# Cross attention's guard moved into the gated experts of a two-layer decoder

## The chip, the cores and the metric

One core of one Trainium2 chip runs the whole program. The metric is the device time of one execution in microseconds, as a median over runs. PE is TensorE, ACT ScalarE, DVE VectorE, POOL GpSimd, SP SyncE, which here only issues transfers.

## What is computed

x has 32 batches of 128 tokens of 128 channels, fp32. Two layers run one after the other, each of an attention, a second attention and a mixture of experts, each added to x. What matters here is the second attention and the first experts:

```
attn = clip(q @ k.T * scale, -1e4, 1e4)
attn = softmax(attn)
attn = where(any(isnan(attn)), 1/Nkv, attn)     # over the whole tensor
x = x + (attn @ v) @ Wo + bo                    # cross attention
x = x + experts(layernorm(x))                   # 8 gated, top 2, and 2 shared experts
```

If any probability is not a number, every output of cross attention becomes the mean of the values, projected. The kernel computes that replacement always, and chooses it by a flag.

## The kernel before

The program is a sequence of blocks. In each, every engine has its own instruction stream, joined to the others by semaphores; between blocks all engines meet. x stays in SBUF as 128 x 4096 (x_all), in 8 groups of 4 batches, 512 columns each. PSUM has 8 banks of 512 columns.

The blocks: the setup, `attention` for self and cross attention together, `uniform_guard` (line 788), `gated_experts` (line 875), `attention` again (causal), `latent_attention`, and `relu_experts` (line 1277), which ends the program.

**In attention** the order on each engine is written out in a table of steps with leads (`ORDERS`, `AHEAD`). SP (lines 778 to 785) copies each group of x into `x_before` as soon as self attention's output is in it, and loads the context of each group. POOL adds the output's bias to x (`add_bias`, L710) after the group has been normalised and, in cross attention, copied. VectorE adds each batch's projected output to x (`add_output`, L663). It also sums the keys and the remainders (`key_sums`, `lo_sums`), from which the guard takes the mean and the flag.

**The guard** runs by itself between the two blocks. It splits the key sums in a rounded and a remaining part (L816, L820), multiplies by the value weights (L845 to L847), makes the mean (ACT, L869) and splits it again, projects it and adds the bias (L831). PE then spreads each batch's row over 128 tokens, one matmul (two passes) per batch, four batches per bank (L861); VectorE adds each bank to `x_before` (L836); and at last one predicated copy of 4096 columns (L840) puts `x_before` in x's place if the flag is set.

**The gated experts** first round their weights (ACT, L1050) and take the remainder (VectorE, L1227). They go by slots: slot n works on group n's five expert pairs (NB = 5, k = 0 to 4), while group n+1 is transposed, split and routed, group n+2 gets its moments and is normalised, and group n-1 is finished. Per k: PE `up` (six matmuls, L950 to L952), `spread_gate` (L977), `down` (L987); ACT silu and a copy of the gate; VectorE their product (L1124); POOL the product with the gate (L1241). The routing is 20 small VectorE operations per group (L1143 to L1174), with one power on POOL in the midst (L1259). PE turns the gates (`transpose_gates`, L1011) at the end of the slot before, ahead of the group's first `up`. Slots -2 to 1 and 6 to 8 are written out; slots 2 to 5 are a loop of two passes over two slots. The bank TR takes the transposes of both x and y; two banks each (H1, H3) take the experts' inputs.

**The end.** The experts of the second layer scatter their weighted rows to `returned` in DRAM, 512 B per row. When all have landed, SP reads them back in 16 transfers (per group and choice, 256 KB each in 512 B pieces, L1454), VectorE adds them to x (L1420, 16 adds), and SP stores the 8 groups (L1458).

## Time and profile before

| | |
|---|---|
| median of 3 runs | 1429.71 us (1428.98 to 1429.92) |
| the profiled execution | 1422.62 us, its span 1420.8 us |
| busy share: PE, DVE, ACT, POOL | 84%, 62%, 48%, 54% |
| mean granted TensorE clock | 0.912 of 2.4 GHz |
| self and cross attention end | 529.49 us |
| guard | to 552.3 us |
| gated experts, last addition to x | 704.49 us |
| last experts, first read of their rows | 1398.67 us |

The table says where the stages lie; how full each is, the windows say. A time in the text is one on the clock of this span.

### The profile page before, as it was taken

Reading aid. Unit: us, or ns where it says so; the run is one execution under the profiler, and the core shown is the slowest. Engines: PE = TensorE matmul, PEld = TensorE weight load, DVE = VectorE, ACT = ScalarE, POOL = GpSimd, SP = SyncE. Lnnn points to the kernel's source line nnn. Section 1 sums busy time; section 2 is a strip of 40 time slices with the busy share of each in tenths; the row PEclk is TensorE's granted clock in tenths of the full one; section 3 lists DMA queues with packets and bytes.
Section 4 is the critical chain, followed back from the end, with each engine's and each line's share of the span. In section 5 each row is a group of like instructions: output and inputs, shape, how many; then the busy total and the mean of one; then the engine's idle time right before and its main releaser. Section 6 shows DMA issues by size and latency. Waiting matters only on the chain. (4 is left out here: it accounts for less than half of the span.)

```text
span 1420.8 us, 34474 instructions
## 1 busy us (share of the span) xinstructions
PE 1192.8 (84%) x12734; PEld 904.7 (64%) x12734; DVE 877.0 (62%) x2007; ACT 675.0 (48%) x1298; POOL 767.3 (54%) x870
## 2 busy tenths in 40 slices
PE   1899998888888875899889999994999994199992
PEld 0577776655555554566457777764899984188881
DVE  3487877589999974666446666555888855022223
ACT  1345544444544531555345454437888532056561
POOL 3677775555566520444365566525776657444552
PEclk9999999789999995999979999996999965599996
DMA  9910000000000000000000000000000001256656
GB/s 347 381 65 10 2 2 15 1 15 28 15 15 8 1 2 1 0 1 0 0 1 3 2 3 2 2 2 23 12 13 2 15 29 49 94 186 206 199 188 181
DMA packets 58865, 75.44 MB, mean 53 GB/s; under 512 B 13246, under 2 KB 40003, under 8 KB 58448
## 3 DMA queue, kind: packets, MB, share of 16 engines
q1 hardware_dynamic: 53328, 63.72, 13.9%
q0 software_dynamic: 4544, 8.47, 1.7%
q8 instruction: 103, 1.69, 0.5%
q10 hardware_dynamic: 832, 1.09, 0.2%
q14 instruction: 58, 0.48, 0.1%
HBM read 40.37 MB, written 31.70 MB: 51 GB/s over the span
## 5 line engine op out<-in xcount | busy, mean ns | idle before, releaser
L590 DVE TENSOR_REDUCE maxes<-bank 128x8 f32<-128x1024 f32 x192 | 234.3, 1221 | 56.3 <-PE bank L392 54.6
L520 ACT ACTIVATE self_probs<-bank 128x1024 f32<-128x1024 f32 x128 | 129.1, 1022 | 46.0 <-PE bank L424 45.6
L1428 POOL DMA_INDIRECT returned<-relu_y,relu_slots x78 | 76.7, 983 | 93.6 <-DVE relu_y L1403 81.1
L1371 ACT ACTIVATE relu_hidden<-bank,cols 128x256 f32<-128x256 f32 x156 | 74.0, 474 | 98.1 <-PE bank L1329 98.1
L527 ACT ACTIVATE self_neg_max<-bank 128x512 fp32r<-128x512 f32 x64 | 38.2, 597 | 155.1 <-PE bank L438 155.1
L731 POOL TENSOR_TENSOR self_k_hi_m<-self_kq_hi,const 128x512 fp32r<-128x512 f32 x64 | 66.6, 1040 | 81.2 <-ACT self_kq_hi L548 81.2
L1329 PE MATMUL bank<-relu_s,relu_w_tile 128*128 128x256 f32 x312 | 94.3, 385 | 0.5 <-DVE relu_s L1397 0.5
L1337 PE MATMUL bank<-relu_hidden,relu_w_tile 128*128 128x256 f32 x312 | 92.9, 381 | 0.0
L1397 DVE COPY relu_s<-bank 128x256 f32<-128x256 f32 x39 | 16.6, 424 | 122.1 <-PE bank L1319 122.1
L600 DVE RECIPROCAL self_recip<-bank 128x128 f32<-128x128 f32 x64 | 61.2, 956 | 32.1 <-PE bank L451 29.8
L596 DVE TENSOR_SCALAR bank<-bank 128x1024 f32<-128x1024 f32 x64 | 78.2, 1223 | 3.3 <-PE bank L412 3.3
L2214 POOL DMA_INDIRECT routed<-latent_rows,latent_place_i x64 | 62.4, 975 | 24.4 <-issue 16.6
L451 PE MATMUL bank<-self_probs,values 128*32 128x128 f32 x2048 | 74.0, 288 | 1.4 <-ACT self_neg_max L527 1.2
L731 POOL TENSOR_TENSOR causal_q_lo_m<-causal_kq_lo,const 128x512 fp32r<-128x512 f32 x32 | 33.3, 1041 | 73.1 <-PE bank L424 73.0
L451 PE MATMUL bank<-self_probs,head_ones 128*32 128x128 f32 x2048 | 71.5, 282 | 0.0
L424 PE MATMUL bank<-self_neg_max,const_r 32*128 32x512 f32 x256 | 63.2, 485 | 9.7 <-DVE bank L596 6.3
L731 POOL TENSOR_TENSOR self_q_lo_m<-self_kq_lo,const 128x512 fp32r<-128x512 f32 x64 | 66.6, 1041 | 2.7 <-PE bank L424 2.7
L451 PEld LDWEIGHTS bank<-self_probs,values 128*32 128x32 f32 x2048 | 55.5, 114 | 18.9 <-issue 16.1
L520 ACT ACTIVATE causal_probs<-bank 128x1024 f32<-128x1024 f32 x64 | 64.5, 1022 | 5.1 <-PE bank L424 2.6
L438 PE MATMUL bank<-ident,maxes 128*128 128x128 f32 x384 | 66.0, 297 | 0.8 <-POOL maxes L754 0.3
L731 POOL TENSOR_TENSOR self_q_hi_m<-self_kq_hi,const 128x512 fp32r<-128x512 f32 x64 | 66.6, 1040 | 0.0
L1337 PEld LDWEIGHTS bank<-relu_hidden,relu_w_tile 128*128 128x128 f32 x312 | 59.5, 191 | 8.3 <-ACT relu_hidden L1371 0.2
(380 smaller groups left out, 3474.9 us busy)
## 6 DMA issues: line engine op xcount, KB each, us to landing
relu_w_tile<-in_w_ffn SPq DMA_DIRECT2D x39, 512.0 KB, 3.4
routed<-blank SPq DMA_DIRECT2D x1, 19760.0 KB, 60.6
relu_slots<-routed SPq DMA_DIRECT2D x39, 130.0 KB, 3.0
relu_back<-returned SPq DMA_DIRECT2D x16, 256.0 KB, 4.5
x_all<-in_x SPq DMA_DIRECT2D x8, 256.0 KB, 8.3
x_before<-x_all SPq DMA_DIRECT2D x8, 256.0 KB, 2.8
out_x<-x_all SPq DMA_DIRECT2D x8, 256.0 KB, 4.2
self_ctx_in<-in_ctx SPq DMA_DIRECT2D x8, 192.0 KB, 2.6
```

The source lines that it names most:

```text
L424: mm = pe.matmul(t_bank(u), cr[rows_of(u), C_ONES + u * P:C_ONES + (u + 1) * P], neg_max[n % 2][rows_of(u), :], start=False, stop=True, sk ...
L438: mm = pe.transpose(OM[:, j * P:(j + 1) * P], maxes[n % 2][:, j * P:(j + 1) * P], sb["ident"][:, :])
L451: mm = pe.matmul(OM[rows_of(u), c:c + P], of(u, j), probs[n % 2][:, u, j, :], start=j == 0, stop=j == U - 1)
L520: act.activation(probs[n % 2][:, 2 * pair:2 * pair + 2, :, :].rearrange("p u j q -> p (u j q)"), T[:, 2 * pair * GT:(2 * pair + 2) * GT], ...
L590: dve.tensor_reduce(out.rearrange("p j u -> p u j"), S.rearrange("p (u j k) -> p u j k", u=2, j=U), AX.X, ALU.max, negate=True).then_inc(m ...
L596: dve.tensor_scalar(t, t, CLAMP / scale, -CLAMP / scale, ALU.min, ALU.max).then_inc(clipped, 1)
L731: pool.tensor_tensor(out[n % 2][:, :, :], src[(n // GB) % 2][:, batch_cols(n)].bitcast(F32).unsqueeze(1).broadcast_to([P, U, P]), slots.un ...
L1329: pe.matmul(HT[i % 2][:, 0:TT], w_tile[t % NW][:, c * P:(c + 1) * P], s[t % 2][:, :], start=True, stop=True)\
L1337: pe.matmul(YT[t % 2][:, 0:TT], w_tile[t % NW][:, F1 + c * P:F1 + (c + 1) * P], hidden[i % C1][:, :], start=c == 0, stop=c == C1 - 1).then ...
L1371: act.activation(hidden[i % C1][:, :], HT[i % 2][:, 0:TT], ACT.Relu, bias=sb["cols"][:, bass.ds(r + (COL_RELU + c), 1)]).then_inc(hidden_d ...
L1428: pool.indirect_dma_start(returned[:, :], bass.IndirectOffsetOnAxis(ap=slots[t % NX][:, b, P:P + 1].bitcast(I32), axis=0), y[t % NY][:, b, ...
L2214: pool.indirect_dma_start(routed[:, :], bass.IndirectOffsetOnAxis(ap=place_i[u % 3][:, k, b:b + 1], axis=0), rows[G % 4][:, k, n % GB, :], ...
```

## The change

1. `uniform_guard` is gone. In attention, ACT ends its program by rounding the key sums (`key_hi`), POOL by taking the remainder (`key_lo`) and the zeros of the flag. VectorE's sums now signal `keys_summed`.
2. SP copies group G to `x_before` after POOL has added the bias, in the order: context G+1, copy of G; each copy waits for the one before. POOL no longer waits for the copy; VectorE's `add_output` does.
3. `gated_experts` begins with the guard. PE makes the mean (into H1) and the flag's sums (H3), then spreads groups 0 to 3 straight from the mean: stationary one column of `v_mean` broadcast to 128, moving `w_out`, so that spreading and projecting are one matmul. They go to four banks that are still free (`EARLY`). VectorE makes the flag, and adds groups 0 and 1 from PSUM; ACT copies groups 2 and 3 to SBUF (`keep_mean`) and POOL adds them (`add_mean`). Groups 4 to 7 are spread in slots 0 to 3 into TR, with the same copy and addition.
4. VectorE chooses a group (`choose`, 512 columns) just before its moments. The weights' remainder is taken after the first moments, and not ahead of all.
5. Group 0's first expert `up` comes ahead of its gates' transpose; that, and two spreads of the gate, come after the second `up`.
6. The loop is written out: `run` is one plain loop over the slots -2 to 8.
7. At the end: `returned` has another order of rows (token p, batch b at p * 32 + b), so that a partition's rows are contiguous; it is read in 8 transfers of 512 KB in pieces of 4 KB, the first choice by SP and the second by ACT; the stores go by SP and ACT in turn.

```diff
@@ attention
+            if "cross" in kinds:
+                act.wait_ge(keys_summed, NG)
+                act.activation(sb["key_hi"][:, :], sb["key_sums"][:, :], ACT.Copy).then_inc(keys_rounded, 1)
...
+                if kind(n) == "cross":
+                    dve.wait_ge(x_kept, 16 * (n // GB - G0 + 1))
                 dve.tensor_tensor(x_of(n), PB[:, 0:P], x_of(n), ALU.add).then_inc(pb_read, 1)
...
             def add_bias(G):
                 pool.wait_ge(xn_done, G + 1)
-                if of_group(G) == "cross":
-                    pool.wait_ge(x_kept, 16 * (G - G0 + 1))
...
+                    if G > 0:
+                        sp.wait_ge(biased, G0 + G)
+                        if G > 1:
+                            sp.wait_ge(x_kept, 16 * (G - 1))
+                        sp.dma_start(x_group(G - 1, "x_before"), x_group(G - 1)).then_inc(x_kept, 16)
@@ gated_experts
+    EARLY = [YT, GATE, H1[1], H3[1]]
...
         def run(engine, slot):
-            for n in range(-2, 2):
+            for n in range(-2, NG + 1):
                 slot(0, n)
-            with engine.Fori(0, 2) as it:
-                for n in range(2, 4):
-                    slot(it, n)
-            for n in range(6, NG + 1):
-                slot(0, n)
...
+            def mean_of_values():
+                pe.wait_ge(ones_set, 1)
+                pe.matmul(H3[0][:, 0:2 * NG], ones[:, :], sb["zeros"][:, :], start=True, stop=True).then_inc(bad_spread, 1)
+                split_matmul(H1[0][:, 0:B], (sb["w_hi"][0:DC, wv:wv + P], sb["w_lo"][0:DC, wv:wv + P]),
+                             (sb["key_hi"][:, :], sb["key_lo"][:, :])).then_inc(mean_made, 1)
+
+            def spread_mean(G):
+                if G == 0:
+                    pe.wait_ge(mean_copied, 1)
+                if G >= len(EARLY):
+                    pe.wait_ge(x_lo_done, G - 2)
+                out = EARLY[G] if G < len(EARLY) else TR
+                for b in range(GB):
+                    n = GB * G + b
+                    mm = pe.matmul(out[:, b * P:(b + 1) * P], v_mean[:, n:n + 1].broadcast_to([P, P]), w_out,
+                                   start=True, stop=True)
+                mm.then_inc(y_spread, 1)
...
+                        if n == 0 and k == 1:
+                            transpose_gates(it, n)
+                            spread_gate(it, n, 0)
+                        if k < NB - 1 and (n, k) != (0, 0):
                             spread_gate(it, n, k)
...
+                    if k == 2 and n >= 0 and there(it, n + 4):
+                        spread_mean(n + 4)
...
+            mean_of_values()
+            for G in range(len(EARLY)):
+                spread_mean(G)
             run(pe, slot)
...
+            keep_mean(2)
+            keep_mean(3)
             run(act, slot)
...
+            def choose(G):
+                columns_of = slice(G * GT, (G + 1) * GT)
+                before = sb["x_before"][:, columns_of]
+                if G < 2:
+                    dve.wait_ge(y_spread, G + 1)
+                    dve.tensor_tensor(before, EARLY[G][:, :], before, ALU.add).then_inc(y_first, 1)
+                    dve.wait_ge(y_first, G + 1)
+                else:
+                    dve.wait_ge(y_added, G - 1)
+                dve.copy_predicated(X[:, columns_of], flag[:, :].broadcast_to([P, GT]), before).then_inc(chosen, 1)
...
+            def add_mean(G):
+                pool.wait_ge(y_mean_read, G - 1)
+                before = sb["x_before"][:, G * GT:(G + 1) * GT]
+                pool.tensor_tensor(before, before, y_mean[G % 2][:, :], ALU.add).then_inc(y_added, 1)
...
+                    if k == 3 and n >= 0 and there(it, n + 4):
+                        add_mean(n + 4)
                     if k >= 1 and there(it, n):
                         gate_hidden(it, n, k - 1)
...
+                    if k == 1 and n == -2:
+                        add_mean(2)
+                        add_mean(3)
@@ relu_experts
+        def load_back(queue, k):
+            rows = returned[k * B * P:(k + 1) * B * P, :].rearrange("(p b) d -> p (b d)", p=P)
+            for H in range(NG // 2):
+                part = slice(2 * H * GT, 2 * (H + 1) * GT)
+                queue.dma_start(back[k][:, part], rows[:, part]).then_inc(back_in[H], 16)
...
+            load_back(act, 1)
+            for G in range(1, NG, 2):
+                store(act, G)
...
+            load_back(sp, 0)
+            for G in range(0, NG, 2):
+                store(sp, G)
```

## Rows read from the trace of the kernel before

**Rows 1.** Windows: length; busy PE, PEld, DVE, ACT, POOL; PEclk; DMA share; GB/s
```profile
529.50:532.80 3.30, 1.05 (x8) 0.83 (x8) 1.32 (x8) 0.52 (x2) 0.21 (x1) 1.00 0.00 0
...
532.80:539.00 6.20, 6.19 (x29) 6.20 (x30) 2.08 (x3) 0.00 (x0) 0.00 (x0) 0.51 0.00 0
...
560.00:571.10 11.10, 3.81 (x16) 3.35 (x16) 5.67 (x30) 2.48 (x6) 2.21 (x3) 0.50 0.01 1
...
589.60:606.10 16.50, 16.50 (x69) 10.31 (x69) 11.01 (x36) 8.68 (x16) 7.25 (x7) 1.00 0.00 0
...
655.40:671.60 16.20, 16.20 (x69) 10.29 (x68) 11.10 (x36) 8.68 (x16) 7.28 (x7) 1.00 0.00 0
```

**Rows 2.** Timeline of the attention's end and the guard: start, us, engine, line, operation
```profile
529.20 0.29 DVE L663 TENSOR_TENSOR x_all<-bank,x_all 128x128 f32<-128x128 f32 x1 [0.58 <-PE bank L464]
...
531.25 0.29 ACT L869 ACTIVATE guard_v_mean<-bank,cols 128x32 f32<-128x32 f32 x1 [6.26 <-PE bank L852]
...
532.81 13.99 PE L861 MATMUL bank<-guard_y,ident 32*128 32x128 f32 x64 [0.37 <-DVE guard_y L831]
...
536.59 0.69 DVE L836 TENSOR_TENSOR x_before<-bank,x_before 128x512 f32<-128x512 f32 x1 [1.01 <-PE bank L861]
...
547.63 4.68 DVE L840 COPY_PREDICATED x_all<-bank,x_before 128x4096 f32<-128x4096 int32 x1
```

**Rows 3.** Timeline of the gated experts' beginning, the same columns
```profile
553.99 1.49 DVE L1227 TENSOR_TENSOR ffn_w_lo<-raw_ffn,ffn_w_hi 128x1280 fp32r<-128x1280 f32 x1 [1.68 <-ACT ffn_w_hi L1050]
...
555.48 0.86 DVE L1184 BATCH_NORM_STATS2 ffn_stats<-x_all 128x6 f32<-128x128 f32 x4
...
558.59 1.65 ACT L1071 ACTIVATE ffn_xn<-x_all,ffn_shift_ln,ffn_rstd 128x128 f32<-128x128 f32 x4 [4.63 <-DVE ffn_shift_ln L1194]
...
568.61 1.65 ACT L1071 ACTIVATE ffn_xn<-x_all,ffn_shift_ln,ffn_rstd 128x128 f32<-128x128 f32 x4 [6.51 <-DVE ffn_shift_ln L1194]
...
570.02 0.16 DVE L1165 TENSOR_TENSOR ffn_two<-ffn_e_second,ffn_two 128x4 f32<-128x4 f32 x1
...
571.17 1.02 PE L1011 MATMUL bank<-ident,ffn_gate_parts 128*16 128x128 f32 x4 [5.57 <-DVE ffn_gate_parts L1174]
...
571.84 0.77 PE L950 MATMUL bank<-ffn_x_hi,ffn_w_hi 128*128 128x512 f32 x1
...
572.22 0.59 ACT L1050 ACTIVATE ffn_g_parts<-bank 16x512 fp32r<-16x512 f32 x1 [1.97 <-PE bank L1011]
...
577.14 0.27 PE L950 MATMUL bank<-ffn_w_hi,ffn_x_hi 128*128 128x8 f32 x1
```

**Rows 4.** Timeline of the second slot, then a line of waits
```profile
601.53 1.29 POOL L1241 TENSOR_TENSOR ffn_hidden<-ffn_product,ffn_gate 128x512 f32<-128x512 f32 x1 [0.22 <-PE bank L987]
...
601.58 1.26 DVE L1165 TENSOR_TENSOR ffn_two<-ffn_e_second,ffn_two 128x4 f32<-128x4 f32 x1
...
PEld bank L1011 <- DVE ffn_gate_parts L1174: 3.0, 5, 0.7
```

**Rows 5.** Timeline of cross attention, then a DMA issue of the page
```profile
487.77 1.28 POOL L710 TENSOR_TENSOR x_all<-x_all,rows 128x512 f32<-128x512 f32 x1
...
513.97 0.29 DVE L663 TENSOR_TENSOR x_all<-bank,x_all 128x128 f32<-128x128 f32 x1 [0.65 <-PE bank L464]
...
x_before<-x_all SPq DMA_DIRECT2D x8, 256.0 KB, 2.8
```

**Rows 6.** Timeline of the end of the program
```profile
1398.67 11.92 SPq L1454 DMA_DIRECT2D relu_back<-returned  x16
...
1402.24 1.42 DVE L1420 TENSOR_TENSOR x_all<-x_all,relu_back 128x512 f32<-128x512 f32 x2 [7.92 <-DMA relu_back<-returned]
...
1409.82 5.95 DVE L1420 TENSOR_TENSOR x_all<-x_all,relu_back 128x512 f32<-128x512 f32 x8 [0.33 <-DMA relu_back<-returned]
```

**Rows 7.** Windows of the loads at the beginning and of the stores at the end
```profile
20.00:40.00 20.00, 9.69 (x26) 6.03 (x26) 6.10 (x21) 5.04 (x11) 7.96 (x13) 1.00 1.05 385
...
1415.80:1418.00 2.20, 0.00 (x0) 0.00 (x0) 0.00 (x0) 0.00 (x0) 0.00 (x0) 0.50 1.15 344
```


## What is expected, and why

> **What bounds the kernel now.** The page's busy shares first (in the table above): PE 84% of the span, VectorE 62%, so work that leaves PE idle is worth removing, and work added to PE where PE is full costs its own length. Then the table of windows [rows 1], to see which of the two holds where the change acts. In the guard (532.8 to 539) PE is full, but at a granted clock of 0.51, the lower of its two levels (1.2 GHz), with only the spreading matmuls in it; from 560 to 571.1, while the first group of the gated experts is routed, PE works 3.8 of 11.1 us at 0.50; in the second group's slot (589.6 to 606.1) PE is busy 16.50 of 16.50 us at 1.00 (2.4 GHz). The four windows after it (16.2 to 16.5 us, the last one shown) are as full. So three stages with three limits: a serial chain (529.5 to about 577), PE (577 to 700), and, at the end of the program, transfers and VectorE's adds (from 1398.7).
>
> **The chain now** [rows 2]. Attention ends at 529.49. The means of the values stand at 531.54. Spreading them over the eight groups takes PE 13.99 us, 1.71 per group; VectorE adds each (0.69) and then chooses all at once in 4.68. Only at 552.3 does the block end, and the gated experts begin [rows 3]: weights split until 555.5, moments at 555.48, normalised x from 558.59, gates ready just before their transpose at 571.17, first expert at 571.84, and the logits' matmuls of the second group from 577.14.
>
> **Change 1: guard inside the gated experts.** Up to 531.54 nothing is saved: the mean still waits for the ones that POOL writes (the flag is now worked out beside it) [rows 2]. From there:
> - First spread: four matmuls of the same output size. 1.71 us at clock 0.50 [rows 2]; PE had 1.00 from 529.5 to 532.8 [rows 1], so half of that, 0.85: done at 532.5. The add 0.69 and an eighth of the choice, 4.68/8 = 0.59 [rows 2], give 534.0 for the first moments instead of 555.48 [rows 3]: 21.5 us earlier.
> - Moments to normalised x took 3.1 us (555.48 to 558.59) [rows 3]: 537.1 at best. Four things now stand in that gap. On VectorE the weight split, 1.49 + 0.16 [rows 3], lies between moments and shift, but beside POOL's power, which has the shift wait for 2.9 us anyway: 0. On ACT the copies of the means of groups 2 and 3 stand ahead of the normalisation; the fourth spread ends between 535.0 (four at 0.85) and 538.4 (at 1.71), with a copy of 0.6 like that at 572.22 [rows 3], so 535.6 to 539.0. On POOL two additions, 1.3 each like its multiplication [rows 4], follow the power. A small VectorE operation beside such a POOL operation takes its length: the product of four columns at 570.02 took 0.16 with POOL idle, the same line at 601.58 took 1.26 and ended with POOL's multiplication [rows 3, 4]. The shift is such an operation, and POOL's addition is queued right behind the power that releases it: one (538.4) or two (539.6) can go first. I take 539.2 for the normalisation, ends 537.1 and 541: 19.4 us earlier.
> - By the Trainium skill (SBUF — State Buffer, Who interferes with whom) that is an exclusive lock between GpSimd and VectorE instructions with two SBUF inputs, and it binds both ways. The rows above agree with the one direction; none shows the other.
> - Then the chain as before: gates ready 12.5 us after the normalisation begins [rows 3]. The second group's add and choice (0.69 + 0.59) and its moments stand on VectorE ahead of the routing, beside the logits' matmuls that it waits for: twelve matmuls in 2.7 us at the lower clock. 0, or 0.2.
>
> **Change 2: the first expert before the gates.** The first expert's six matmuls (2.6 at the lower clock: 571.84 to the next work at 574.3, the last of them faster) now run under the routing. But next on PE's queue is the transpose of the second group, which waits for its normalisation, 10.0 us after the first (568.61 less 558.59) [rows 3] plus 1.65; everything behind it waits too. So: 11.7, transpose 0.7 to 1.1, second expert 1.4 (clock 1.00) to 2.6 (0.50), gates' transpose, ACT copy, spread, ACT copy, spread 3.2 to 3.5 with PE idle between: second logits at 17.0 to 18.9 after the normalisation, before 18.55 (577.14 less 558.59) [rows 3]. The reordering gives 1.5 to -0.3, and the lower clock could cost those logits another 1.3. I take 18.1, 0.4 gained. Front in sum: 557.3 instead of 577.1, **-19.8** (ends -23.0 and -16).
>
> **Change 3: four spreads, copies and adds in four slots.** In slots 0 to 3 PE is full, so each spread costs 0.85 there. Its ACT copy (0.6) falls under the next expert. POOL's addition (as long as a multiplication, 1.29) comes ahead of the third expert's multiplication, which is done when the fourth's begins at 601.53 [rows 4]. The last routing steps are VectorE operations that wait behind POOL as above, and PE already waits for them: 3.0 us in the five slots from 589, 0.7 at most [rows 4]. Followed through: the last multiplication then runs until 603.9, and the product of four columns ends with it instead of at 602.84; the gates are 1.1 later while PE comes 0.85 later. So 1.1 per slot, **+4.4** for four; 3.4 if the routing finds gaps, 8.8 if it loses one more POOL operation in each. The choice of a group (0.59) is in six slots on VectorE, 11.0 busy of 16.5 [rows 1], in the gap before the logits: 0.
>
> **Change 4: the loop written out.** The four looped slots keep the pace of the others (16.2 to 16.5), so **-0.2**, between 0 and -0.5.
>
> **Change 5: x kept after the bias is added, and VectorE waits for it.** SP's copy of a group now follows that group's bias on POOL. The last bias is at 487.77, the first output of that group is added at 513.97, and a copy lands 2.8 us after its issue [rows 5]: 22 us to spare, so 0. The context load of a group is queued behind a copy two groups older, whose bias comes earlier still: 0. The rounding of the key sums stands at the end of ACT's and POOL's programs, while VectorE still has the last outputs to add: 0.
>
> **Change 6: the end.** Now one queue issues 16 loads in 11.92 us, one per 0.75, and the first store waits behind them; VectorE's first add is at 1402.24, 3.6 after the first issue, for 0.5 MB, and its last eight take 5.95, 0.74 each [rows 6]. From 1398.7 on 6.29 MB move (24 transfers of 256 KB) in 512 B pieces, at 344 GB/s where nothing else binds. The transfers at 20 to 40 us, in long pieces, went at 385 GB/s [rows 7]. New: two queues, 4 KB pieces, first pair of 1 MB after 2.2 + 2.7 (3.6 less 1.4 for 0.5 MB, and 1 MB at 385) = 1403.6; 16 adds of 0.74 end at 1415.5, last store 0.75 issue + 2.5 to land: 1418.8. By data: 4.19/385 + 2.10/344 = 17.0 us from 1399.6, 1416.6, which is earlier. So **-2.0**; 0 if the first pair comes 2 us later, -3.2 if the last store lands in 1.3. The new scatter addresses change no size: 0. The Trainium skill (DMA: Bandwidth & Descriptors, Issuing engines are not separate DMA queues) has all queues on the same 16 engines, so that a second one saves only issue time; by its limit of HBM per core, about 358 GB/s, the loads would take 11.7 us instead of 10.9, against 385 measured here.
>
> **Sum.** -19.8 + 4.4 - 0.2 - 2.0 = -17.6 us. The profiled execution took 1422.62 (span 1420.8 and 1.8 around it): 1405.0. The three timed runs have a median of 1429.71, 7.1 above it, which the trace doesn't place; taken off there: **1412.1**.
>
> **Rivals.**
> - POOL's power is held by the weight split (1.49), which starts while the power is due: the normalisation is 1.4 later, 1413.5. For it: the order on VectorE, and that POOL can hold VectorE in this way [rows 3, 4]. Against it: no row shows POOL held. Chance 0.25. The Trainium skill's rule (SBUF — State Buffer, Who interferes with whom) would have it so.
> - The slots cost more: one more POOL operation before the routing's end in each slot, 8.8 instead of 4.4, and the second expert at the lower clock, +1.7: 1418.2. For it: PE already waits 0.6 per slot for the gates. Chance 0.13.
> - Front at its fast end: no addition before the shift and clock 1.00 for the spreads: -3: 1409. Chance 0.17.
> - The change does less than it says: if a fifth and later spread had to be done before the experts begin, each would cost 1.7; the code puts four ahead. 1419; 0.02.
> - Slower: in cross attention the wait for the kept copy. If each copy were issued only when the group's first output is due, VectorE, with the maxima of the next batch queued behind, would stand 2.8 us and PE behind it, eight times: +22.4, 1434.5. It decides from 2.2 us per group. Against it 22 us of slack. Chance 0.02.
> - The forecast: 0.40; another 0.01 that all cancels.
>
> Range: 1406.5 (fast front with a fast end of the program) to 1418.5. A measurement of this kernel tells about 0.2% (2.9 us) from no change: faster 0.97, same 0.01, slower 0.02.
>
> **What would show it.** First moments near 534 and normalisation near 539 after an unchanged 529.5; second logits near 557; slots 0 to 3 of about 17.5 us and slots 4 and 5 of 16.4; additions on POOL right before VectorE's long small operations; last adds ending near 1415.3 less the shift. Wrong would be: a normalisation after 541, slots over 18.5, or an attention stage that ends later than 530.

## The result, and the profile after

The changed kernel takes 1424.25 us (median of 20 runs, 1419.47 to 1443.25) beside 1434.53 us for the kernel before in the same comparison (median of 20): a ratio of **0.9932, 95% interval 0.9917 to 0.9947**, or 9.7 us less (the medians lie 10.3 apart). A few runs at a much lower mean clock stand outside the ratios: here the one of 1443.25 us (clock 0.865), later one of `unrolled` (1987.85) and one of `after_third` (1433.27). The forecast was 1412.1 us, 17.6 less: the direction holds, the size is little more than half. The profiled execution took 1423.83 us, its span 1422.0.

The guard's place in the trace after, beside [rows 2, 3]. Columns: start, us, engine, line, operation, out<-in.

```profile
531.23 0.61 PE L942 MATMUL bank<-zeros,ffn_ones 128*128 128x16 f32 x2 [1.32 <-POOL ffn_ones L1294]
...
532.51 0.29 ACT L1089 ACTIVATE ffn_v_mean<-bank,cols 128x32 f32<-128x32 f32 x1 [6.67 <-PE bank L885]
...
532.85 5.87 PE L955 MATMUL bank<-w_out,ffn_v_mean 128*128 128x128 f32 x32 [0.38 <-ACT ffn_v_mean L1089]
535.04 0.69 DVE L1173 TENSOR_TENSOR x_before<-bank,x_before 128x512 f32<-128x512 f32 x1 [2.80 <-PE bank L955]
535.76 0.73 DVE L1177 COPY_PREDICATED x_all<-ffn_flag,x_before 128x512 f32<-128x512 int32 x1
536.53 0.87 DVE L1186 BATCH_NORM_STATS2 ffn_stats<-x_all 128x6 f32<-128x128 f32 x4
...
537.84 1.46 DVE L1206 TENSOR_TENSOR ffn_w_lo<-raw_ffn,ffn_w_hi 128x1280 fp32r<-128x1280 f32 x1
...
538.11 1.25 POOL L1263 TENSOR_SCALAR ffn_var_eps<-ffn_mean_var 128x4 f32<-128x4 f32 x1 [6.86 <-DVE ffn_mean_var L1190]
...
539.44 1.04 POOL L1266 TENSOR_TENSOR ffn_rstd<-ffn_var_eps,ffn_power 128x4 f32<-128x4 f32 x1
540.45 2.48 POOL L1277 TENSOR_TENSOR x_before<-x_before,ffn_y_mean 128x512 f32<-128x512 f32 x2
540.51 1.22 DVE L1196 SCALAR_TENSOR_TENSOR ffn_shift_ln<-ffn_mean_var,ffn_rstd 128x4 f32<-128x4 f32 x1 [1.13 <-POOL ffn_rstd L1266]
541.76 0.88 ACT L1041 ACTIVATE ffn_xn<-x_all,ffn_shift_ln,ffn_rstd 128x128 f32<-128x128 f32 x2 [2.41 <-DVE ffn_shift_ln L1196]
```

Attention ends at 530.24 in this trace, 0.75 later than in the one before. The first moments are at 536.53 instead of 555.48, the first normalisation at 541.76 instead of 558.59, the second logits' products at 559.80 instead of 577.14. Two operations of four columns are long here: POOL's addition to the variances (1.25) beside VectorE's split of the weights, and VectorE's shift (1.22) beside POOL's addition of the mean.

The granted clock of this stretch and of the beginning of causal attention, in the trace after. Columns: window, length, busy PE (instructions), PEclk, DMA share, GB/s.

```profile
529.10:532.60 3.50, 1.74 (x7) 0.67 0.00 0
532.80:536.50 3.70, 3.65 (x17) 0.50 0.00 0
536.50:541.80 5.30, 2.22 (x17) 0.94 0.00 2
...
694.50:700.50 6.00, 0.78 (x4) 0.75 0.01 3
700.50:712.50 12.00, 7.90 (x26) 0.50 0.00 0
712.50:718.50 6.00, 5.44 (x19) 0.50 0.00 0
718.50:724.50 6.00, 6.00 (x38) 0.50 0.01 3
724.50:736.50 12.00, 12.00 (x78) 0.50 0.00 1
736.50:742.50 6.00, 6.00 (x78) 0.55 0.01 3
```

The same windows of causal attention in the kernel before, counted from its first moments at 704.8:

```profile
704.80:710.80 6.00, 0.76 (x4) 0.68 0.00 0
710.80:722.80 12.00, 7.92 (x26) 0.50 0.00 1
722.80:728.80 6.00, 5.42 (x19) 0.50 0.00 0
728.80:734.80 6.00, 5.49 (x50) 0.83 0.01 3
734.80:752.80 18.00, 17.84 (x263) 1.00 0.01 3
```

TensorE's instructions are the same, in the same order, and for the first 24 us they start at the same times. Before, the clock then rises, 26 us in; after, it stays at 0.50 (1.2 GHz) for 21 us more, with PE busy 12.00 of 12.00 us. Nothing in causal attention was changed, and it is 8.4 us longer. No step of the forecast dealt with it.

The end of the program after, to be read beside [rows 6]:

```profile
1402.35 1.93 SPq L1339 DMA_DIRECT2D relu_back<-returned  x4
1402.36 2.05 ACTq L1339 DMA_DIRECT2D relu_back<-returned  x4
...
1407.54 10.84 DVE L1461 TENSOR_TENSOR x_all<-x_all,relu_back 128x512 f32<-128x512 f32 x16 [9.51 <-DMA relu_back<-returned]
```

Eight loads are issued in 2 us, the first addition comes 5.2 us after the first issue, and the sixteen run back to back.

**Stages.** Of each kernel that ran there is one trace; the names are explained with the experiments. The table has the stages of the two kernels, their repetitions and three with a part of the change (us; the first column runs from VectorE's last multiplication in cross attention, 1.2 ahead of its end, to the first moments of causal attention; the second to latent attention's beginning; the last from the first load of the returned rows to the end of the span).

| trace | guard and experts | causal | latent | last experts | end |
|---|---|---|---|---|---|
| before | 176.5 | 255.6 | 278.1 | 160.2 | 22.1 |
| before_again | 183.9 | 255.6 | 287.0 | 160.8 | 21.6 |
| tail_only | 183.7 | 255.5 | 290.8 | 160.6 | 19.6 |
| unrolled | 183.8 | 255.5 | 283.8 | 160.5 | 21.8 |
| after | 165.4 | 264.0 | 283.0 | 160.9 | 19.7 |
| after_again | 165.3 | 264.0 | 289.4 | 161.2 | 19.7 |
| after_third | 166.2 | 264.0 | 279.3 | 161.3 | 19.7 |
| front_only | 165.9 | 264.0 | 282.9 | 160.8 | 23.0 |

Latent attention takes 278 to 291 with the old front and 279 to 289 with the new, and explains nothing. The other columns give the change: 165.7 - 183.8 = -18.1 in the first (four traces with the new front, the three like ones with the old), +8.4 in the second, +0.5 in the fourth, -2.0 to -2.5 in the last: about -11.4, where the runs gave -9.7. (The first two traces, 1420.8 and 1422.0 in span, show no gain at all: the one of before is 7.3 short in the first column, and 4.8 are latent attention's.)

### The profile page after: what moved, and what is told of

It is laid out like the page before. It is cut to its first block and busy times, and to the rows that moved or that the text cites. A ratio compares the mean times of both kernels' runs of the same rounds, so it can differ in the third digit from the quotient of the medians.

```text
span 1422.0 us, 34178 instructions
## 1 busy us (share of the span) xinstructions
PE 1198.5 (84%) x12731; PEld 905.0 (64%) x12731; DVE 879.4 (62%) x2002; ACT 677.7 (48%) x1304; POOL 775.9 (55%) x878
## 5 line engine op out<-in xcount | busy, mean ns | idle before, releaser
L2249 POOL DMA_INDIRECT routed<-latent_rows,latent_place_i x64 | 62.9, 982 | 29.8 <-issue 16.9
L451 PEld LDWEIGHTS bank<-self_probs,values 128*32 128x32 f32 x2048 | 55.5, 115 | 19.2 <-issue 16.3
L438 PEld LDWEIGHTS bank<-ident,maxes 128*128 128x128 f32 x384 | 43.8, 148 | 33.8 <-issue 27.9
```

The lines of the kernel that those rows point to most:

```text
L438: mm = pe.transpose(OM[:, j * P:(j + 1) * P], maxes[n % 2][:, j * P:(j + 1) * P], sb["ident"][:, :])
L451: mm = pe.matmul(OM[rows_of(u), c:c + P], of(u, j), probs[n % 2][:, u, j, :], start=j == 0, stop=j == U - 1)
L2249: pool.indirect_dma_start(routed[:, :], bass.IndirectOffsetOnAxis(ap=place_i[u % 3][:, k, b:b + 1], axis=0), rows[G % 4][:, k, n % GB, :], ...
```

## The experiments

**Both kernels again, and the two halves of the change.**

> The kernel before, unchanged, for a second trace. Theory A (the half-clock stretch at the start of causal attention is chance): its length differs from the 24 us of the first trace by several us, and causal and latent attention together take other than 534.2 us (704.8 to 1239.0) by up to 10. Theory B (it belongs to the program): it is within 2 us of 24, and the two stages within 2 of 534.2. The time against the kernel before: ratio 1.000 in both.

> The changed kernel, unchanged, for a second trace. Theory A (chance): the half-clock stretch in causal attention isn't the 42 us of the first trace (700 to 742) and causal and latent attention take other than the 547.4 us there by up to 10. Theory B (moved there by the change): it is near 42 again and the two stages near 547. The stage of guard and gated experts takes 164.3 us (530.2 to 694.5) within 1.5 by both. Ratio 0.993 in both.

`front_only` is the changed kernel with the old end; `tail_only` is the old kernel with the new end:

```
-  sp: 16 loads relu_back[k][G] <- returned, then 8 stores      (L1454 before)
+  load_back(sp, 0), load_back(act, 1); store(sp, even G), store(act, odd G)
+  C_HOME: row of x numbered B * p + b instead of P * b + p
```

> The change without its last part: the rows are read back in 16 transfers by one queue and stored by it, as before. Theory A: the front alone is worth 11.0 us less 0.7 of attention, 0.9928; the end of the program takes 22.1 us as before. Theory B (part of the front's gain is given back in causal attention): 7 us, 0.995, and the half-clock stretch there is long again. If the end were worth nothing, this would be equal to the whole change, 0.993.

> The kernel before with only the last part of the change: rows in the new order, read in 8 transfers of 4 KB pieces by two queues, stored by two. Forecast by the windows: the end takes 19.6 instead of 22.1 us, ratio 0.9982. Rival (the rows scattered 16 KB apart slow the experts' loop or the last scatter): the loop is longer by 0.5 to 1 us and the ratio is 0.999 or above.

Ratios to before, in the order of the four texts above: 1.0019 [0.9999, 1.0039], 0.9934 [0.9907, 0.9961], 0.9927 [0.9901, 0.9953], 0.9983 [0.9962, 1.0004]. The gain is all but wholly the front's. The end is 2.0 to 2.5 us shorter in tail_only's own trace and 2.3 us in its median, at the edge of what these runs tell; with the new front the runs don't show it at all (front_only, without it, has 0.9927, the whole change 0.9934), though in the traces the end takes 23.0 us there and 19.7 with it. As to chance or program: causal attention's length is the program's, 255.5 or 255.6 in every trace of the table with the old front and 264.0 in every one with the new. The sums with latent attention, by which theory B was to be told too, missed (542.6 for 534.2 and 553.4 for 547.4), because latent attention alone differs by that much from trace to trace. And front_only met the time of its theory A with the long stretch of its theory B: the front is worth more than I thought, and causal attention takes it back.

The trace that the forecast rests on is the odd one of its kernel. In the first column it has 176.5, and the others 183.7 to 183.9: their clock rises later, and from the first to the second logits they take 16.9 instead of 13.0, from the second to the third 19.6 to 19.8 instead of 16.9. Their clock is lower from attention's end on. These are the windows of `before_again` and `tail_only` that answer to 529.5 to 532.8 in [rows 1], with the same columns (1.00 there; `unrolled` has 0.51 and `warm_before` 0.50):

```profile
532.97:536.27 3.30, 1.41 (x7) 1.35 (x8) 1.04 (x7) 0.52 (x2) 0.20 (x1) 0.58 0.00 0
...
524.61:527.91 3.30, 1.42 (x7) 1.36 (x8) 1.04 (x7) 0.52 (x2) 0.20 (x1) 0.51 0.00 0
```

**The loop alone** (`unrolled`):

```
-            for n in range(-2, 2): slot(0, n)
-            with engine.Fori(0, 2) as it: for n in range(2, 4): slot(it, n)
-            for n in range(6, NG + 1): slot(...)
+            for n in range(-2, NG + 1): slot(0, n)
```

> The kernel before with the gated experts' loop written out and nothing else. In the three traces with the old guard, causal attention lasted 255.5 to 255.6 us from its first moments to latent attention's beginning, and in the three with the new one 264.0. Theory P: the clock of TensorE at causal attention's beginning rises early or late by how the work lies in time, and written-out code alone doesn't move it: causal attention 255.6 us, and the whole within 0.1% of before (slots of the gated experts 0.0 to 0.2 us shorter at the two loop ends). Rival U: the written-out code is what moved it (its last slots run a little otherwise): causal attention 264.0, and the whole about 8 us slower than before (ratio 1.006).

Ratio 1.0003 [0.9985, 1.0021], causal attention 255.5, slots of 16.35 to 16.37 us from the second on (16.28 to 16.57 in the looped kernel). Theory P stands, U is out: written-out code neither costs nor gives anything, and it doesn't move the clock.

**Keeping TensorE at work in causal attention's beginning** (`warm_before` on the old kernel, `warm` on the new one):

```
+            def keep_warm(n):
+                for _ in range(n):
+                    pe.matmul(T[:, 3 * GT:4 * GT], cr[:, C_ID:C_ID + P], cr[:, 0:GT], start=True, stop=True)
+            # 20 ahead of step ("x", 0); 5, 3, 3, 5, 3 behind ("x",0) ("k",0) ("q",0) ("s0",0) ("x",1)
```

> The kernel before, with 39 products without use (128x128 by 128x512, into the bank that holds the key scores and is free until then) in TensorE's gaps at the beginning of causal attention: 20 ahead of the first transposes, 5, 3, 3, 5 and 3 later. Theory P: the granted clock stays at 1.00 there instead of 0.50 for 24 us, and causal attention falls from 255.6 to 246 to 250 us; whole ratio 0.993 to 0.997. Rival Q: products without use don't hold the clock, or cost as much as they give: 255 to 258 us.

> The changed kernel with the same 39 products at the beginning of causal attention. Theory P (the 8.4 us that causal attention lost are the clock's alone, 0.50 for 44 us instead of 24): causal attention falls from 264.0 to the same length as in the kernel before with these products, 246 to 250 us, within 0.5 us of it; ratio to before 0.981 to 0.985, some 12 to 17 us faster than the change alone. Rival Q (something else of the change slows causal attention): it falls by what the kernel before falls by, and stays 8 us longer than there.

`warm`: **0.9831 [0.9807, 0.9855]**, causal attention 250.0 us; once more (`warm_again`) 0.985 [0.9814, 0.9886] and again 250.0. No window of its first 56 us is below 1.00. So 14.0 us of causal attention come back by nothing but products whose result nobody reads: the 8.4 us are the clock's. `warm_before`: 0.9964 [0.9937, 0.9992], 254.6 us, where 246 to 250 were expected, and so not the same length as `warm` either. The low stretch wasn't gone but put off:

```profile
711.00:735.00 24.00, 21.83 (x133) 1.00 0.00 1
735.00:741.00 6.00, 5.84 (x58) 0.93 0.00 1
741.00:749.00 8.00, 8.00 (x90) 0.50 0.01 2
```

With the 39 products the clock stays up in four traces (`warm`, `warm_again`, `best`, `best2`: 250.0 us) and falls once, 29 us in and for 7 to 10 us, in four others (`warm_before`, `warm_late`, `late_add_warm`, `best2_again`: 253.0 to 254.6). What decides isn't explained; the kernel `best2` did both.

> The same kernel as warm, once more, beside the three above on one chip: the ratio to before 0.981 to 0.986 again, causal attention 250 to 253 us again. If causal attention were now 264, the 39 products had not been the cause.

**Split of the weights behind the shift** (`late_split`):

```
-                    if k == 0 and n == -2: split_weights()          # VectorE
+                    if k == 3 and n == -2: split_weights()
-                    if k == 1 and n == -2: add_mean(2); add_mean(3) # POOL
+                    if k == 1 and n == -1: add_mean(2); add_mean(3)
```

> The changed kernel with VectorE's split of the experts' weights behind the first shift instead of ahead of it, and GpSimd's first two additions of the mean one slot later, behind the second deviation. Theory L (the two engines keep each other from SBUF: GpSimd's addition to the variances took 1.25 us beside the split instead of 0.20, VectorE's shift 1.22 beside the addition instead of 0.16): both fall to 0.2 us, first moments to first normalisation takes 2.8 to 3.4 us instead of 5.2, and the first logits are read 2 us sooner after attention's end (17.2 instead of 19.2); whole ratio to before 0.990 to 0.993. Rival: the logits wait for the split instead, or the rounding of the weights on ScalarE ends later than the normalisation could begin: within 0.5 us of the change.

```profile
533.51 0.20 POOL L1263 TENSOR_SCALAR ffn_var_eps<-ffn_mean_var 128x4 f32<-128x4 f32 x1 [6.85 <-DVE ffn_mean_var L1190]
533.79 1.04 POOL L1266 TENSOR_TENSOR ffn_rstd<-ffn_var_eps,ffn_power 128x4 f32<-128x4 f32 x1
...
534.87 0.16 DVE L1196 SCALAR_TENSOR_TENSOR ffn_shift_ln<-ffn_mean_var,ffn_rstd 128x4 f32<-128x4 f32 x1 [1.54 <-POOL ffn_rstd L1266]
```

Theory L holds: 0.20 and 0.16 instead of 1.25 and 1.22, moments to normalisation 3.14 us instead of 5.23, first logits 17.6 us after the last multiplication of attention instead of 19.2. But the second logits come 32.4 us after it in both, since the two additions now hold the routing (two operations of 0.19 us took 1.01 and 1.18), and the stage is 167.1 us, 1.7 longer. The ratio is nevertheless 0.9885 [0.986, 0.9911], because causal attention took 255.6 us. Here is its clock:

```profile
691.60:693.60 2.00, 0.00 (x0) 1.00 0.03 8
693.60:715.60 22.00, 14.15 (x48) 0.50 0.00 0
715.60:719.60 4.00, 3.48 (x18) 0.76 0.00 0
719.60:723.60 4.00, 4.00 (x50) 1.00 0.02 4
```

So the long low stretch isn't tied to the new front either. In the twelve traces without warming products: where the clock fell 1.7 to 2.2 us after causal attention's first moments (before, before_again, tail_only, unrolled, late_split, late_add), it stayed low for 24 us; where it fell 2.9 to 3.1 us after (after, after_again, front_only, no_steady, spread_early, after_third), for 44. An edit 150 us earlier goes with one or the other; whether the moment of the fall is the cause or only a sign of it, and what sets it, isn't shown.

> The kernel late_split with the 39 products without use at the beginning of causal attention. Theory P (what causal attention lost or kept is the granted clock's alone): in late_split it had the shorter length already, 255.6 us, and with these products it comes to what the changed kernel had with them, 250.1 us, so the two edits together give less than their sum: 5.5 us more than late_split, a ratio to before of 0.982 to 0.986. Rival: the two add up in full (late_split's 8.4 us came from elsewhere): a ratio of 0.974 to 0.979.

`warm_late`: 0.9856 [0.9817, 0.9894], causal 253.0 instead of the 250.1 expected. The two edits don't add up, as P has it, though the clock was kept only up to the 29th us.

**What the slots cost.** `no_steady` leaves out the mean of groups 4 to 7; `spread_early`, built on `late_split`, makes their products ahead of the slots:

```
-                    if k == 2 and n >= 0 and there(it, n + 4): spread_mean(n + 4)   # both
-                    if k == 3 and n >= 0 and there(it, n + 4): add_mean(n + 4)      # no_steady alone
+  spread_early: spread_mean(4) behind transpose_x(0), spread_mean(5..7) behind up(0, 0); six y_mean tiles
```

> The changed kernel without the mean of groups 4 to 7: their products, their copy from the bank and GpSimd's addition are left out, so where the guard chose the replaced output these four groups would lack it; the predicated copies stay. It prices the slots. Theory T (the 1.16 to 1.9 us that each of slots 0 to 3 lost are TensorE's 0.9 us of spreading products, since TensorE bounds the slot, and the 0.5 us that it waits for gates held up by GpSimd's addition): without them slots 0 to 3 fall to 16.35 to 16.7 us, as slots 4 and 5 of the change, and the stage from attention's end to the first causal moments shortens by 4.5 to 5.5 us. Rival K: the predicated copy is what costs (it lengthens VectorE's order ahead of the routing), and the slots keep 0.8 us or more each of what they lost. The whole, with the granted clock's part of it open: ratio to before 0.984 to 0.991.

> The kernel late_split with the products of groups 4 to 7 made ahead of the steady slots, in TensorE's gaps of the beginning (one group behind the first transposes, three ahead of the second), each copied into a tile of its own; GpSimd's additions stay in slots 0 to 3. Theory T: slots 0 to 3 lose TensorE's 0.9 us each and keep up to 0.5 us of waiting for gates: 16.4 to 16.9 us instead of 17.7; the beginning keeps its length if the gaps are real (or grows by up to 1.5 us at the lower clock). Attention's end to the first causal moments 163 to 165 us instead of 167.1. Causal attention takes one of its two lengths (255.6 or 264.0) by how its beginning lies in time, which this theory can't place. Rival K: slots 17.3 or more, since the products weren't what they lost.

`no_steady`: slots 1 to 3 took 16.83, 16.64, 16.67 instead of 17.93, 17.71, 17.71, nearly as T has it; the stage didn't shorten (166.2), since slot 0 went at the lower clock (21.9 instead of 18.8), and the ratio is 0.9921 [0.989, 0.9951]. `spread_early`: 17.93, 17.70, 17.71, **unchanged though the products are gone**, so T falls. The stage is 172.9 us where 163 to 165 were expected, with a ratio of 0.9968 [0.9941, 0.9996]: TensorE then stood idle in one piece (1.58 busy of 7.50) and the next 20 us went at 0.50. The third slot, first of `spread_early` (busy PE, PEld, DVE, ACT, POOL; then PE's wait), then of the changed kernel:

```profile
607.59:625.29 17.70, 16.78 (x69) 10.19 (x69) 13.74 (x38) 8.68 (x16) 8.49 (x9) 1.00 0.00 0
...
PE bank L974 <- DVE ffn_gate_parts L1167: 0.9, 1, 0.9
```

```profile
598.19:615.90 17.71, 17.39 (x77) 11.16 (x77) 12.87 (x37) 9.28 (x17) 8.50 (x10) 1.00 0.00 0
...
PE bank L972 <- DVE ffn_gate_parts L1163: 0.3, 1, 0.3
```

PE wins 0.6 us of work and waits 0.6 longer for the gates. What holds the gates is seen in the routing of the changed kernel, above, and of `unrolled`, below, which have the same operations:

```profile
585.37 1.27 POOL L1277 TENSOR_TENSOR x_before<-x_before,ffn_y_mean 128x512 f32<-128x512 f32 x1
...
586.60 2.52 POOL L1254 TENSOR_TENSOR ffn_hidden<-ffn_product,ffn_gate 128x512 f32<-128x512 f32 x2
...
586.91 0.99 DVE L1154 TENSOR_TENSOR ffn_two<-ffn_e_second,ffn_two 128x4 f32<-128x4 f32 x1
587.93 1.27 DVE L1156 TENSOR_TENSOR ffn_shares<-ffn_one_hot,ffn_two 128x64 f32<-128x64 f32 x1
...
589.92 0.19 DVE L1163 TENSOR_TENSOR ffn_gate_parts<-ffn_gates,ffn_gate_parts 128x32 fp32r<-128x32 f32 x1 [0.21 <-DVE ffn_gate_parts L1161]
```

```profile
622.46 1.29 POOL L1236 TENSOR_TENSOR ffn_hidden<-ffn_product,ffn_gate 128x512 f32<-128x512 f32 x1 [0.22 <-PE bank L982]
622.51 1.26 DVE L1160 TENSOR_TENSOR ffn_two<-ffn_e_second,ffn_two 128x4 f32<-128x4 f32 x1
623.80 0.23 DVE L1162 TENSOR_TENSOR ffn_shares<-ffn_one_hot,ffn_two 128x64 f32<-128x64 f32 x1
...
624.57 0.19 DVE L1169 TENSOR_TENSOR ffn_gate_parts<-ffn_gates,ffn_gate_parts 128x32 fp32r<-128x32 f32 x1
```

From the logits' read (580.26 and 616.49) to the last part of the gates 9.85 us against 8.27: POOL's three long operations stand in a row and hold two VectorE operations behind the power, where there was one. (A third, of 0.90, is held near the routing's start by a multiplication; `late_add`, below, has it too.)

**The addition out of the routing** (`late_add`, with the weights' split behind the shift as well; with the warming products `late_add_warm`, and with 18 more in the experts' beginning `best2`):

```
+                    if k == NB - 1 and n >= 0 and there(it, n + 3):
+                        pool.wait_ge(routed, RS * (n + 2)); add_mean(n + 3)
+                    if k == 1 and n == -2: pool.wait_ge(split_lo, 1); add_mean(2)
+  best2: keep_warm(LG, 6) behind the first four spreads, keep_warm(YT, 12) behind up(0, 0)
```

> The changed kernel with GpSimd's additions of the mean moved out of the routing: group 2's behind the split of the weights, those of groups 3 to 7 one slot's end later, behind a wait for the routing of that slot; the split of the weights behind the first shift. Theory R (the slots' 1.35 us are the routing's: from the logits' read to the last part of the gates VectorE took 9.85 us in the changed kernel and 8.27 in the one before, because operations of 0.2 us took 0.9 to 1.3 beside GpSimd's addition): the routing falls to 8.3 to 8.9 us, TensorE's wait for gates is gone, and slots 1 to 3 fall to where TensorE's own work bounds them, 16.36 + 0.9 of products = 17.2 to 17.3 us. Rival K (the predicated copy and its order): 17.6 to 17.7. Attention's end to the first causal moments 162 to 165.5 us. Causal attention 255.6 or 264.0, which this theory can't place.

> late_add with the 39 products without use at causal attention's beginning. Theory P: causal attention 250 to 253 us whatever late_add's was, and the whole 1.5 to 3 us below the changed kernel with these products alone: ratio to before 0.979 to 0.984. Rival: no better than warm.

> late_add_warm with 18 more products without use in the gated experts' beginning: 6 behind the first spreading, into the logits' bank, and 12 behind the first up projections, into the bank of the sums. If they hold the granted clock at 1.00 from the spreading on, the first slot (20.4 us in late_split, 18.8 in the change, 16.9 in one trace of before) is 17 to 18.5 us, and attention's end to the first causal moments is 2 to 4 us below late_add's: ratio to before 0.976 to 0.982. Rival: they delay the second transposes or the clock falls all the same: no better than late_add_warm, or 1 us worse.

```profile
622.69 0.18 DVE L1152 RECIPROCAL ffn_two<-ffn_total 128x4 f32<-128x4 f32 x1
622.90 0.16 DVE L1154 TENSOR_TENSOR ffn_two<-ffn_e_second,ffn_two 128x4 f32<-128x4 f32 x1
623.10 0.23 DVE L1156 TENSOR_TENSOR ffn_shares<-ffn_one_hot,ffn_two 128x64 f32<-128x64 f32 x1
...
624.14 1.28 POOL L1277 TENSOR_TENSOR x_before<-x_before,ffn_y_mean 128x512 f32<-128x512 f32 x1 [1.51 <-DVE ffn_gate_parts L1163]
```

`late_add`: slots 1 to 3 took 17.25, 17.26, 17.26 us, where theory R said 17.2 to 17.3, and the routing 7.8 us (616.30 to 624.06). That decides it: each slot has two limits, TensorE's 17.26 with the products and the routing's 17.7 with the addition, and the later one counts. The predicated copy doesn't make the 17.7. A smaller part stays open: without any addition, in slots 4 and 5 of the changed kernel and in slots 2 to 5 of `no_steady`, a slot still takes 16.64 to 16.70 us instead of 16.36, two VectorE operations are held (1.24 and 1.00 us) and the routing takes 8.6 us instead of 8.3. Slot 4 of `late_add` copies a group too and takes 16.37, so the copy's 0.8 us alone doesn't explain that either.

Stage 164.0, causal 255.5, ratio 0.9877 [0.9831, 0.9923]; `late_add_warm` 0.988 [0.984, 0.992] where 0.979 to 0.984 was expected, no better: its clock fell 29 us into causal attention (254.6). `best2`: 0.9835 [0.9794, 0.9877] for an expected 0.976 to 0.982; the stage took 160.6 us, 3.3 below late_add's, but not where I had put it: the first slot took 20.2 us and most of the gain lies ahead of it (first logits at 15.7 instead of 17.6 us). Of those 1.9 us, 1.4 came before any of the 18 products, by a clock that fell later (first moments 4.85 us after attention's end instead of 6.29, as in `after_again`, which has no such product). In a second run (`best2_again`) the first moments were at 6.29 again and the stage took 160.4 us, so the products are worth the 3.3 to 3.6 us of it.

**Everything at once.** `best` is spread_early with the warming products and 11 more in the front; it took 0.9851 [0.9817, 0.9885], with a stage of 173.1 us where 158 to 163 were expected, 12.5 longer than best2's. The 11 products didn't keep the clock: it was at 0.50 from 25.8 to 49.7 us after attention's last multiplication, as in `spread_early` (25.7 to 49.6).

> spread_early with the 39 products at causal attention's beginning and 11 more in the experts' beginning, into the bank of the logits (2 ahead of the mean of the values, 3 behind it, 6 behind the first four groups' products). If the clock's granting follows TensorE's full products, the experts' beginning keeps 1.00 longer and attention's end to the first causal moments takes 158 to 163 us, causal attention 250.1 us: ratio to before 0.976 to 0.982. Rival: the products come where the engine is on the path at the lower clock and delay the first normalisation's transposes, and the ratio is no better than that of the changed kernel with the 39 products alone, 0.983.

> The same kernel as best2. From attention's end to the first causal moments 160 to 162 us, causal attention 250 us, ratio to before 0.980 to 0.986.

> The changed kernel once more beside best2: ratio to before 0.991 to 0.996, causal attention 264.0 us a fourth time if its length belongs to the program, 255.5 us if it is chance; and 10 to 18 us longer than best2.

On one chip, `best2` took 1405.38 us, 0.9849 [0.9813, 0.9885], and the changed kernel 1412.74 (the median of the five runs that count), 0.9901 [0.9867, 0.9936]: 7.4 apart, less than the 10 to 18 expected, though the two traces differ by 15.2 in the stages that best2 touches (160.4 + 254.6 against 166.2 + 264.0). best2's stage came as expected (160.4), its causal attention didn't (254.6 for 250). With six and five runs, that spread over 13 and 10 us, and with intervals that overlap, this isn't decided. By their first comparisons `best2` (0.9835) and `warm` (0.9831) are faster than the changed kernel (0.9932 [0.9917, 0.9947]); the two can't be told from each other.

## Why the prediction was wrong in size

The forecast failed at four steps: it put causal attention at nothing without a reason, it sized the slots too small, it took the clock of the first spread from a stretch that happened to be fast, and it took an odd trace as its base. The last error helped, by luck, and hid more than half of what the others cost.

**The base.** The 7.1 us between the profiled execution and the median were "taken off" as lying outside the change. As far as the traces show they lay inside it: in four traces of five with the old guard the first slots went at the lower clock and the stage took 7.2 to 7.4 us more. Against the profiled execution the stage gained 11.1 us (176.5 to 165.4), against the usual one 18.

**First moments, 534.0: 1.8 late** once the 0.75 of attention's end is off. The step that failed is "PE had 1.00 from 529.5 to 532.8, so half of that, 0.85". The changed kernel had 0.67 and 0.50 there; the mean stood 0.5 later after attention's end, and the first group's spread took 2.19 up to its addition. One trace's clock was taken for the program's: of the old kernel's five traces four have 0.50 to 0.58 there. In `after_again` the clock happened to be at 1.00, the spread took 1.27 and the first moments came 4.85 us after attention's end (forecast 4.5, this trace 6.29). The choice took 0.73, not the 0.59 of an eighth of the long one.

**Moments to normalisation, 5.2: measured 5.23**, by a different sum. The forecast had one of POOL's additions ahead of the shift; the rows show that, at 1.22, and besides POOL's small addition held for 1.25 by the split, the first rival's lock in the direction that no row had shown, though on another operation than the power. By the Trainium skill (SBUF — State Buffer, Who interferes with whom) the lock binds both ways; here the trace agrees, 1.25 against 0.20 us.

**Second logits, 18.1 after the normalisation: measured 18.04.** The second group's transpose came after 11.2 instead of 11.7, the second expert took 2.7 at the lower clock, the long end of its range. The third expert (six products from 561.29, the clock 0.51 from 561 to 564.5) went at the lower clock too and made slot 0 dearer.

**The slots, +4.4: measured +5.9 in slots 0 to 3** (1.9, 1.45, 1.36, 1.16) **and +0.7 in 4 and 5**, for which I had said 0. The mechanism was named rightly, "the last routing steps wait behind POOL" and "the gates are later", and late_add shows it; the term was mis-sized: two operations held, not one, so that the routing took 9.6 to 9.9 us instead of 8.3 and a slot 1.4 us more instead of 1.1. That is the mechanism of the second rival at less than its 8.8 us. In slots 4 and 5 two operations are held as well, though POOL adds nothing there. The loop, -0.2, is in the slots' differences already.

**The end, -2.0: measured -2.0 to -2.5.** The first pair came 5.2 us after its issue where 4.9 was worked out, the sixteen adds took 10.84 instead of 11.84, and the program ended 3.6 us after them instead of 3.25: the size is right in part because these cancel. The rate was read amiss: from 24 us on the traffic in the first window of [rows 7] is no load but the one transfer that writes `routed` (19,760 KB, from SBUF). The loads of the returned rows themselves went at 389 GB/s (1404.5 to 1407.5) and 422 (1407.5 to 1410.5).

**What was missing: +8.4 in causal attention.** The failed step is one that isn't there: no step of the forecast dealt with anything behind the stage that changed, which puts those stages at nothing. The profile before had what was needed to see the risk, if not the sign: right behind the change 24 us at half the clock, with TensorE at work for 16.1 of them. In these two traces the stage gave 11.1 where the forecast had 15.6 (19.8 + 0.2 - 4.4), causal attention took 8.4 back, and the end gave 2.5. That the clock makes the 8.4 is shown by `warm` and `late_split`; what sets how long it stays low is open.

Of the rivals on the wait for the kept copy and on a later spread nothing is seen: attention's last multiplication lies at 523.4 to 531.8 us in the five traces with the old front and at 523.7 to 529.1 in the four of the change and of its front alone, and in the trace after no engine waits for a copy into `x_before`. Two of the signs for "wrong" came true with little weight: attention ended after 530 (530.24), which is within what the old kernel does (524.6 to 533.0), and slot 0 was over 18.5 (18.79), by its clock. The third, a normalisation after 541, came with 541.76 and named a real miss.

## What to carry to other kernels

Before pricing an edit, take a second profile of the unchanged kernel: a stage whose length differs between two traces of one program is no base for a sum, least of all its short one. After an edit, compare stage by stage over the whole program, also where nothing was edited: here the granted clock differed, by 8.4 us of time, in a stage 150 us behind the edit. Where a stage has two limits close together, taking work from the one engine only turns into waiting for the other; what decides is found by taking away each alone.

## What the runs showed of the hardware

- PE was busy 12.00 of 12.00 us at a granted clock of 0.50 in causal attention, some two thirds of it with products of 32 and 64 rows, and 6.19 of 6.20 at 0.51 in the old guard [rows 1]. The same kinds of products ran at 1.00 in the kernel before (734.8 to 752.8). In the changed kernel it rose at 537.1 us, 4.3 us after the new spreading, of 128 rows, had begun. What made the difference isn't shown.
- At causal attention's beginning a low stretch lasted 24 us in six traces and 44 in six others, behind the same work.
- 39 products that nobody reads were worth 14.0 us of causal attention to the changed kernel and 1.0 to the one before.
- A two-input operation of VectorE and one of POOL held each other in both directions: POOL's small addition took 1.25 us instead of 0.20 beside VectorE's split, VectorE's shift 1.22 instead of 0.16 beside POOL's addition. Where three POOL operations of 1.27 us stood in a row behind the power, two small VectorE operations were held.
- A predicated copy of 128x512 took 0.72 to 0.80 us, the eight of the changed kernel 6.1, where one of 128x4096 took 4.68 [rows 2].
